# Layer 0's expert scatter in a two-layer transformer kernel: one fp32 product per token block, or two float32r products of a split row

## The chip, the cores and the metric

The kernel runs on one core of a Trainium2 chip, as one program and one launch. The metric is device microseconds of one execution. Engine names are those of the profile: PE is the matmul engine, PEld its weight loads, DVE the vector engine, ACT the scalar engine, POOL the GpSimd engine, SP the engine that issues most plain DMAs.

## What is computed

Two transformer layers over x of shape (8, 512, 128), with adaptive layer norms. Layer 0 is softmax attention and an expert layer in which each expert takes its own best tokens; layer 1 is linear attention and a top-2 expert layer. The change is in layer 0's expert layer:

```python
scores = jnp.einsum('ntd,ed->nte', x, gate_w)
probs = jax.nn.softmax(scores, axis=-1)
g, m = jax.lax.top_k(probs.transpose(0, 2, 1), k)      # 8 experts, k = 128 of 512 tokens
xin = x[batch_idx, m]
h = jnp.einsum('nekd,edf->nekf', xin, w1)
h = jax.nn.gelu(h, approximate=False)
h = jnp.einsum('nekf,efd->nekd', h, w2)
out_tok = g[..., None] * h
out = jnp.zeros((n, t, d), dtype=x.dtype).at[batch_idx, m].add(out_tok)
```

and x becomes x + gb * out, with gb a gate per batch and feature.

## The kernel before, in words

The program has three parts. `program_attention` does layer 0's attention for all 8 batches and the choice of each expert's tokens. `program_experts` begins with a pipeline of stages, one batch wide, in which three batches are in work at once: layer 0's experts of batch nn = b + 2, layer 1's attention of batch nxt = b + 1, and layer 1's routing of batch b. After it come 72 tiles of layer 1's experts and an output part. The change touches only the pipeline.

A stage is cut into Q = 32 slots, and the order is written by hand. On each engine a table `work[q]` lists functions by slot; slot after slot they are issued in the order in which they were appended, and the engine runs them in that order. Expert e of the stage occupies slots from 4e on:

- PE: `hidden0(e+1)` in slot 4e (4 products of 128x128x128, L1852), `output0(e)` in slot 4e+1 (4 products into bank `tb`, L1860), `scatter(e-1)` in slot 4e+2 (4 products, L1870). The last expert's `scatter(7)` runs in slot 2 of the next stage. An fp32 product stands in the trace as two weight loads and two matmuls, so 4 products are x8.
- ACT: `gelu0(e+1)` in slot 4e+1 (L1374).
- DVE: `spread_picks(e)` in slot 4e makes a 128x512 matrix of zeros and ones (L1549): which token each of the expert's 128 rows belongs to. `save_y0(e)` in slot 4e+2 reads `tb`, multiplies by the token weight and the gate and writes `y0[e % 2]` (L1558).

`scatter(e)` multiplies, for each of 4 token blocks, a 128x128 quarter of `spread` (as weights) by `y0` and accumulates over the 8 experts in bank `a2`. `start_b` (DVE, slot 3, L1523) adds that bank to x, and takes the statistics of layer 1's first norm (L1490, L1495).

Other work that the prediction speaks of, with its slots: on PE `norm2_T` in 5 (L1821), `logits` in 7 and `shared` in 8 (both L1826), `norm1_T` in 9 (L1821), `values` in 15 (L1826), `ranks` in 18 (L1971 to L1976, waits for `combT_ready`), `contexts` in 19 (L1914). On ACT `save_hTf` in 6 (L1413; `logits` waits for it), `shift_1` in 10 (L1380), `exp_router` in 11 (L1418), `q_positive` in 13 (L1392), `gelu_shared` in 15 (L1422), `exp_qk` and `save_v1` in 16 (L1396 to L1403), `save_combT` in 18 (L1427). ACT loads a table each time it goes from gelu to exp or back. On DVE `norm_f` in 31 (L1541), `q_negative` in 14 and `k_negative` in 15.

The stages differ in what runs beside the experts. The first has the experts alone, the second also layer 1's attention, and in both DVE does one round of `take_best` per expert (slot 4e+1: MAX8, FIND_INDEX8, MATCH_REPLACE8 over 512 columns) for the last two batches. Six more have experts, attention and routing; two after these have no layer 0 experts.

Of the kernel before, what the change touches and what calls it, by code (L numbers as in the profile page):

```python
# [14 lines left out]
F32 = mybir.dt.float32  # L15
BF16 = mybir.dt.bfloat16
F32R = mybir.dt.float32r
I32 = mybir.dt.int32
U32 = mybir.dt.uint32
ALU = mybir.AluOpType  # L20
# [3 lines left out]
P = 128  # L24
B, T, D = 8, 512, 128
# [4 lines left out]
E, F = 8, 512  # L30
# [934 lines left out]
def program_experts(nc, io, keep, scratch, held):  # L965
# [4 lines left out]
    with ctx:  # L970
        def sb(name, shape, dt=F32):
            return ctx.enter_context(nc.sbuf_tensor(name, shape, dt))
# [4 lines left out]
        def sem(name):  # L977
            held.append(nc.alloc_semaphore(name=name))
            return held[-1]
# [10 lines left out]
        def column(name, rows=P):  # L990
# [18 lines left out]
        xg = sb("xg", [P, E, D])  # L1009
        xin = sb("xin", [P, E, KSEL])  # L1010
        hid0 = [sb(f"hid0_{i}", [P, NF, KSEL]) for i in range(2)]
        spread = [sb(f"spread{i}", [P, T]) for i in range(2)]
        y0 = [sb(f"y0_{i}", [P, D]) for i in range(2)]

        st_b = sb("st_b", [P, NT, 6])
        mv_b = sb("mv_b", [P, NT, 2])
# [90 lines left out]
        a2 = pb("a2", [P, T])  # L1107
# [16 lines left out]
        g_filled, xin_ready, z0_filled, hid0_ready, spread_ready, y0_filled, y0_ready, sc_filled, x0_ready = (  # L1124
            sem(n) for n in "g_filled xin_ready z0_filled hid0_ready spread_ready y0_filled y0_ready sc_filled "
            "x0_ready".split())

        stb_done, mvb_done, rb_step, rsb_ready, xhb_ready, hT1_filled, hT1_ready = (
            sem(n) for n in "stb_done mvb_done rb_step rsb_ready xhb_ready hT1_filled hT1_ready".split())
# [55 lines left out]
        def quarter(t):  # L1185
            return slice(P * t, P * (t + 1))
# [170 lines left out]
        def _(act):  # L1357
            def iteration(it):
                b, nxt, nn = it.own, it.own + 1, it.own + 2
# [10 lines left out]
                def gelu0(m, e):  # L1370
                    act.wait_ge(z0_filled, E * m + e + 1)
                    if e >= 2 or not (isinstance(m, int) and m == 0):
                        act.wait_ge(y0_filled, E * m + e - 1)
                    nc.scalar.activation(hid0[e % 2][:].rearrange("p n k -> p (n k)"), ps_h[e % 2][:], ACT.Gelu  # L1374
                                         ).then_inc(hid0_ready, 1)

                def shift_1():
                    act.wait_ge(hT1_filled, nxt + 1)
                    act.wait_ge(q1_filled, nxt)
                    nc.scalar.activation(hT1[:], b0_[:], ACT.Identity, scale=scale1[:, 1, 0, bass.ds(nxt, 1)],  # L1380
                                         bias=mod[:, 1, SHIFT_A, bass.ds(nxt, 1)]).then_inc(hT1_ready, 1)
# [47 lines left out]
                work = {q: [] for q in range(Q)}  # L1429
                if it.ffn:  # L1430
                    if not it.attn:
                        work[0] += [lambda: gathered(0, 0), lambda: gathered(0, 1), lambda: gelu0(0, 0)]
                    for e in range(E - 1):
                        work[4 * e + 1].append(lambda e=e: gelu0(nn, e + 1))
                    if it.ffn_next:
                        work[24].append(lambda: gathered(nn + 1, 0))
                        work[29].append(lambda: gelu0(nn + 1, 0))
                        work[31].append(lambda: gathered(nn + 1, 1))
# [46 lines left out]
        def _(dve):  # L1485
# [32 lines left out]
            def iteration(it):  # L1518
                b, nxt, nn = it.own, it.own + 1, it.own + 2
# [32 lines left out]
                def save_y0(e):  # L1552
                    dve.wait_ge(y0_filled, E * nn + e + 1)
                    if e >= 2 or not (isinstance(nn, int) and nn == 0):
                        dve.wait_ge(sc_filled, E * nn + e - 1)
                    dve.wait_ge(gate0_in, 16)
                    settle(dve)
                    nc.vector.scalar_tensor_tensor(y0[e % 2][:], tb[:, 0:D], weight_of[:, nn, e:e + 1],  # L1558
                                                   gate0[:, nn, :], ALU.mult, ALU.mult).then_inc(y0_ready, 1)

                def take_last(n):
                    if n == 0:
# [166 lines left out]
                if it.ffn and not it.route:  # L1729

                    for n in range(ROUNDS // 2):
                        work[4 * n + 1].append(lambda n=n: take_last(ROUNDS // 2 * (b + 2) + n))
                    if it.attn:
                        work[29] += [place_last, save_earlier]
                        work[31].append(keep_last)
                for q in range(Q):
                    for f in work[q]:
                        f()
# [79 lines left out]
        def _(pe):  # L1818
# [10 lines left out]
            def iteration(it):  # L1829
# [32 lines left out]
                    last.then_inc(y0_filled, 1)  # L1862

                def scatter(m, e):
                    pe.wait_ge(y0_ready, E * m + e + 1)
                    pe.wait_ge(spread_ready, E * m + e + 1)
                    if e == 0:
                        pe.wait_ge(x0_ready, m)
                    for t in range(NT):
                        last = nc.tensor.matmul(a2[:, quarter(t)], spread[e % 2][:, quarter(t)], y0[e % 2][:],  # L1870
                                                start=(e == 0 and t == 0), stop=(e == E - 1), skip_group_check=True)
                    last.then_inc(sc_filled, 1)

                def picks_T(which, n):
# [298 lines left out]
```

## Time and profile before

| | |
|---|---|
| median of 3 runs | 1170.81 us (1170.74 to 1175.88) |
| the profiled execution, its own time | 1174.08 us |
| its span from first to last instruction | 1172.4 us |
| mean granted TensorE clock | 0.901 |
| PE / PEld / DVE / ACT / POOL busy | 84% / 53% / 65% / 49% / 38% |
| pipeline stages with layer 0 experts | about 588 to 888 us |

A row of the trace's timeline gives start, duration, engine, line, operation, output and inputs, and in brackets how long the engine had been idle and which instruction released it. Matmuls overlap: the mean duration of one (278 ns for L1870) is not its cost in a stream. The cost is the distance from the start of one group to the start of the next.

### The profile page before, as it was taken

The numbers are of one execution on the slowest core, as the hardware profiler recorded it, in microseconds if no ns is written. First come the engines' busy times: TensorE is split into PE (matmuls) and PEld (weight loads), VectorE is DVE, ScalarE is ACT, GpSimd is POOL, SyncE is SP. The second block draws the span as 40 slices with busy tenths as digits, with TensorE's granted clock in tenths as the row PEclk, the third lists the DMA queues.
The fourth block names the chain that finished last, engine by engine and source line by source line (L and its number), as shares of the span: only waits on it lengthen the run. The fifth ranks groups of instructions, "written<-read, shape, count | busy, mean of one in ns | idle before, by whom it ended". The sixth has DMA issues, their size and how long they took to land.

```text
span 1172.4 us, 21238 instructions
## 1 busy us (share of the span) xinstructions
PE 981.7 (84%) x6249; PEld 616.0 (53%) x6249; DVE 766.4 (65%) x1912; ACT 579.6 (49%) x1225; POOL 444.3 (38%) x625
## 2 busy tenths in 40 slices
PE   4699999999899999994198999999996539999764
PEld 3133333333233333332197888889885439999621
DVE  3668787878687878896188756665665336656333
ACT  1057676767576767771023533552453116666421
POOL 4030414131222222121324565665534336666532
PEclk9569999999899999996599999999998559999876
DMA  4432323232232324510600010100101012222232
GB/s 141 140 120 75 132 72 131 74 128 76 100 105 97 106 96 108 186 49 10 277 19 19 20 31 27 31 26 22 33 8 48 18 33 68 65 68 68 82 92 75
DMA packets 55645, 90.11 MB, mean 77 GB/s; under 512 B 9393, under 2 KB 40539, under 8 KB 54902
## 3 DMA queue, kind: packets, MB, share of 16 engines
q1 hardware_dynamic: 45942, 58.68, 17.5%
q0 software_dynamic: 9600, 30.24, 7.2%
q8 instruction: 42, 0.69, 0.3%
q14 instruction: 61, 0.50, 0.1%
HBM read 49.62 MB, written 39.30 MB: 76 GB/s over the span
## 4 chain that ended last, share of the span: by engine, by line
PE 34%; DVE 6%; DMA 3%; issue 3%; POOL 3%; ACT 3%; SPq 0%; DVEq 0%; ACTq 0%; POOLq 0%
PE a L2030 6%; PE tb L1860 5%; PE a L1852 4%; PE a L1870 4%; PE b_ L2039 3%; PE c L1826 2%; PE a L2039 2%; PE b_ L1826 2%; DMA weights<-back_dram 1%; DMA xg<-tokens_dram,row_of 1%; PE b_ L1922 1%; PE b_ L1821 1%; ACT L1418 1%; PE b_ L1914 1%; POOL rows_dram L1303 1%
## 5 line engine op out<-in xcount | busy, mean ns | idle before, releaser
L630 DVE TENSOR_REDUCE nmax<-ps_s 128x1 f32<-128x512 f32 x512 | 324.8, 683 | 87.7 <-PE ps_s L795 86.5
L524 ACT ACTIVATE p_ring<-ps_t 128x512 f32<-128x512 f32 x512 | 287.2, 597 | 141.6 <-PE ps_t L806 138.1
L817 PE MATMUL ps_av<-p_ring,v_ext 128*32 128x512 f32 x1024 | 138.8, 615 | 0.0
L795 PE MATMUL ps_s<-weights 72*128 72x512 bf16 x256 | 108.3, 427 | 19.5 <-DMA weights<-q_parts_dram 15.6
L1466 ACT ACTIVATE weights<-a,wtile 128x128 f32<-128x128 f32 x288 | 82.3, 368 | 49.5 <-PE a L2030 49.5
L1330 POOL DMA_INDIRECT back_dram<-weights,target x72 | 84.0, 1167 | 57.8 <-DVE weights L1783 51.9
L806 PE MATMUL ps_t<-weights 75*128 75x512 bf16 x256 | 102.0, 398 | 2.6 <-ACT p_ring L524 1.5
L806 PE MATMUL ps_t<-q_stack,k_stack 75*128 75x512 bf16 x256 | 96.7, 382 | 3.9 <-ACT p_ring L524 2.0
L795 PE MATMUL ps_s<-k_stack,q_stack 72*128 72x512 bf16 x256 | 98.1, 383 | 1.3 <-DVE nmax L630 1.3
L1374 ACT ACTIVATE hid<-a 128x512 f32<-128x512 f32 x64 | 38.2, 597 | 112.5 <-PE a L1852 112.3
L1303 POOL DMA_INDIRECT rows_dram<-hrow,slot x64 | 63.2, 988 | 64.5 <-DVE slot L1690 46.1
L1852 PE MATMUL a<-xin,weights 128*128 128x128 f32 x512 | 74.7, 292 | 7.8 <-ACT xin L1366 7.8
L2030 PE MATMUL a<-hTt,wtile 128*128 128x128 f32 x576 | 78.4, 280 | 3.1 <-ACT hTt L1457 3.1
L1261 POOL DMA_INDIRECT xg<-tokens_dram,row_of x64 | 63.4, 990 | 38.0 <-DVE row_of L1513 18.9
L795 PEld LDWEIGHTS ps_s<-weights 72*128 72x128 bf16 x256 | 26.0, 102 | 97.1 <-DVE nmax L630 55.3
L2030 PEld LDWEIGHTS a<-hTt,wtile 128*128 128x128 f32 x576 | 71.5, 195 | 5.6 <-ACT hTt L1457 4.8
L1769 DVE COPY wtile<-wall 128x1028 f32 x72 | 56.7, 787 | 27.1 <-issue 26.5
L1852 PEld LDWEIGHTS a<-xin,weights 128*128 128x128 f32 x512 | 65.4, 200 | 16.7 <-issue 8.6
L1860 PE MATMUL tb<-weights,hid 128*128 128x128 f32 x512 | 72.0, 286 | 2.5 <-DVE y L1558 1.8
L1860 PEld LDWEIGHTS tb<-weights,hid 128*128 128x128 f32 x512 | 66.6, 202 | 7.5 <-issue 4.7
L455 POOL CAST m_parts<-nmax 128x16 bf16<-128x16 f32 x32 | 6.3, 198 | 167.1 <-DVE nmax L630 167.1
L1870 PE MATMUL a<-y,spread 128*128 128x128 f32 x512 | 68.6, 278 | 0.7 <-DVE y L1558 0.7
(286 smaller groups left out, 1681.2 us busy)
## 6 DMA issues: line engine op xcount, KB each, us to landing
rows_dram<-wmod POOLq DMA_DIRECT2D x8, 2145.0 KB
q_parts_dram<-q_parts SPq DMA_DIRECT2D x40, 128.0 KB, 2.4
xt<-rows_dram SPq DMA_DIRECT2D x72, 65.0 KB, 1.8
weights<-k_parts_dram SPq DMA_DIRECT2D x16, 288.0 KB
weights<-q_parts_dram SPq DMA_DIRECT2D x16, 288.0 KB
k_stack<-k_parts_dram SPq DMA_DIRECT2D x16, 288.0 KB
q_stack<-q_parts_dram SPq DMA_DIRECT2D x16, 288.0 KB
wall<-in_wall SPq DMA_DIRECT2D x1, 4112.0 KB, 20.7
```

Of the source, the lines that this page charges most:

```text
L524: nc.scalar.activation(probs[:, u % RING, :], ps_t[u % TBANKS][:], ACT.Exp, scale=HD ** -0.5).then_inc(exp_done, 1)
L630: nc.vector.tensor_reduce(nmax[:, js, n:n + 1], ps_s[u % SBANKS][:], AX.X, ALU.max, negate=True).then_inc(max_done, 1)
L795: nc.tensor.matmul(ps_s[u % SBANKS][:], q_stack[par][0:STACK, h, quarter(t)], k_stack[par][0:STACK, h, :], start=True, stop=True).then_inc ...
L806: nc.tensor.matmul(ps_t[u % TBANKS][:], k_stack[par][0:STACK + PARTS, h, quarter(t)], q_stack[par][0:STACK + PARTS, h, :], start=True, sto ...
L817: last = nc.tensor.matmul(ps_av[32 * g:32 * (g + 1), :], v_ext[par][:, t, HG * j + g, :], probs[:, (HG * k + g) % RING, :], start=(t == 0) ...
L1303: nc.gpsimd.indirect_dma_start(out=scratch["rows"].ap(), out_offset=bass.IndirectOffsetOnAxis(ap=slot[:, k, t:t + 1], axis=0), in_=hrow[:, ...
L1330: nc.gpsimd.indirect_dma_start(out=scratch["back"].ap(), out_offset=bass.IndirectOffsetOnAxis(ap=target[j % YT][:, 0:1], axis=0), in_=yt[j ...
L1466: last = nc.scalar.activation(hid1[j % 2][:, n, :], ps_z[j % 2][:, quarter(n)], ACT.Gelu, bias=wtile[j % WT][:, 2 * F + n:2 * F + n + 1])
L1852: last = nc.tensor.matmul(ps_h[e % 2][:, quarter(f)], w1_0[:, e, quarter(f)], xin[:, e, :], start=True, stop=True)
L1860: last = nc.tensor.matmul(tb[:, 0:D], hid0[e % 2][:, f, :], w2_0[:, e, f, :], start=(f == 0), stop=(f == NF - 1))
L1870: last = nc.tensor.matmul(a2[:, quarter(t)], spread[e % 2][:, quarter(t)], y0[e % 2][:], start=(e == 0 and t == 0), stop=(e == E - 1), ski ...
L2030: last = nc.tensor.matmul(ps_z[j % 2][:, quarter(n)], wtile[j % WT][:, quarter(n)], hTt[j % 2][:], start=True, stop=True)
```

## The change

Each expert's 128x128 rows `y0` are split in two float32r tiles. ACT copies `y0` into the first (`high_y0`), which rounds it; DVE subtracts that from `y0` into the second (`low_y0`). `spread` becomes float32r too (zeros and ones). The scatter makes two float32r products per token block, high and low, into the same quarter of `a2`, and waits for the low part. In the compiled program a float32r product is one weight load and one matmul, and an fp32 product is two of each.

```diff
-        spread = [sb(f"spread{i}", [P, T]) for i in range(2)]
+        spread = [sb(f"spread{i}", [P, T], F32R) for i in range(2)]
         y0 = [sb(f"y0_{i}", [P, D]) for i in range(2)]
+        y0_parts = [sb(f"y0_parts{i}", [P, 2, D], F32R) for i in range(2)]
...
+                def high_y0(e):
+                    act.wait_ge(y0_ready, E * nn + e + 1)
+                    nc.scalar.copy(y0_parts[e % 2][:, 0, :], y0[e % 2][:]).then_inc(y0_high_ready, 1)
...
                         work[4 * e + 1].append(lambda e=e: gelu0(nn, e + 1))
+                    for e in range(E):
+                        work[4 * e + 2].append(lambda e=e: high_y0(e))
...
+                def low_y0(e):
+                    dve.wait_ge(y0_high_ready, E * nn + e + 1)
+                    nc.vector.tensor_tensor(y0_parts[e % 2][:, 1, :], y0[e % 2][:],
+                                            y0_parts[e % 2][:, 0, :].bitcast(F32), ALU.subtract
+                                            ).then_inc(y0_low_ready, 1)
...
+                if it.ffn:
+                    for e in range(E):
+                        work[4 * e + 3].append(lambda e=e: low_y0(e))
...
                 def scatter(m, e):
-                    pe.wait_ge(y0_ready, E * m + e + 1)
+                    pe.wait_ge(y0_low_ready, E * m + e + 1)
                     pe.wait_ge(spread_ready, E * m + e + 1)
...
                     for t in range(NT):
-                        last = nc.tensor.matmul(a2[:, quarter(t)], spread[e % 2][:, quarter(t)], y0[e % 2][:],
-                                                start=(e == 0 and t == 0), stop=(e == E - 1), skip_group_check=True)
+                        for c in range(2):
+                            last = nc.tensor.matmul(a2[:, quarter(t)], spread[e % 2][:, quarter(t)],
+                                                    y0_parts[e % 2][:, c, :], start=(e == 0 and t == 0 and c == 0),
+                                                    stop=(e == E - 1 and c == 1), skip_group_check=True)
```

The instructions of PE keep their order. On ACT and DVE the two new ones stand at hand-written places. In the changed kernel's rows line numbers are higher: by 2 to 6 on ACT, by 8 to 14 on DVE.

ACT, first routed stage, slots 1 to 10, before (`hid` is `gelu0`, `hT_f` is `save_hTf`, `hT` is `shift_1`):

```order
L1374 ACTIVATE hid_1<-a 128x512
L1374 ACTIVATE hid_0<-a 128x512
L1413 COPY hT_f<-c 128x512
L1374 ACTIVATE hid_1<-a 128x512
L1380 ACTIVATE hT<-b_,mod,scale 128x512
```

and now (`y_parts` is `high_y0`):

```order
L1376 ACTIVATE hid_1<-a 128x512
L1381 CAST y_parts<-y_0 128x128
L1376 ACTIVATE hid_0<-a 128x512
L1381 CAST y_parts<-y_1 128x128
L1419 COPY hT_f<-c 128x512
L1376 ACTIVATE hid_1<-a 128x512
L1381 CAST y_parts<-y_0 128x128
L1386 ACTIVATE hT<-b_,mod,scale 128x512
```

The casts of expert 1 and expert 2, which wait for DVE, now stand directly ahead of `hT_f` and `hT`.

ACT, the same stage, slots 13 to 18, before (`q_pos` is `q_positive`, `sh` is `gelu_shared`, `combT` is `save_combT`):

```order
L1392 ACTIVATE q_pos<-b_,small 128x512
L1422 ACTIVATE sh<-sh 128x512
L1396 ACT_TABLE_LOAD
L1396 ACTIVATE q_exp<-q_exp 128x512
L1398 ACTIVATE k_exp<-k_exp 128x512
L1403 COPY v<-b_ 128x4x128
L1374 ACT_TABLE_LOAD
L1374 ACTIVATE hid_1<-a 128x512
L1427 COPY combT<-c 8x512
```

and now:

```order
L1398 ACTIVATE q_pos<-b_,small 128x512
L1381 CAST y_parts<-y_1 128x128
L1428 ACTIVATE sh<-sh 128x512
L1402 ACT_TABLE_LOAD
L1402 ACTIVATE q_exp<-q_exp 128x512
L1404 ACTIVATE k_exp<-k_exp 128x512
L1409 COPY v<-b_ 128x4x128
L1376 ACT_TABLE_LOAD
L1376 ACTIVATE hid_1<-a 128x512
L1381 CAST y_parts<-y_0 128x128
L1433 COPY combT<-c 8x512
```

Expert 3's cast stands ahead of `sh` and the table load, and expert 4's ahead of `combT`.

DVE, the first routed stage, slots 2 to 8, now (`y_0` and `y_1` are `save_y0`, `y_parts` is `low_y0`, `x` with `st_b` and `mv_b` is `start_b`); before, the order is the same without the two `y_parts` rows:

```order
L1566 SCALAR_TENSOR_TENSOR y_0<-tb,weight_of,gate 128x128
L1521 TENSOR_TENSOR row_of<-token_of,tokens 128x8
L1531 TENSOR_TENSOR x<-a,x 128x512
L1498 BN_STATS st_b<-x 128x6 x4
L1503 BN_AGGR mv_b<-st_b 128x2 x4
L1571 TENSOR_TENSOR y_parts<-y_0,y_parts 128x128
L1557 TENSOR_SCALAR spread<-tokens,token_of 128x512
L1566 SCALAR_TENSOR_TENSOR y_1<-tb,weight_of,gate 128x128
L1571 TENSOR_TENSOR y_parts<-y_1,y_parts 128x128
L1557 TENSOR_SCALAR spread<-tokens,token_of 128x512
```

Expert 0's subtraction comes only after the whole of `start_b`.

## Rows read from the trace of the kernel before

**Rows 1.** The page: busy time, granted clock in 40 slices, the chain by line.

```profile
PE 981.7 (84%) x6249; PEld 616.0 (53%) x6249; DVE 766.4 (65%) x1912; ACT 579.6 (49%) x1225; POOL 444.3 (38%) x625
...
PEclk9569999999899999996599999999998559999876
...
PE a L2030 6%; PE tb L1860 5%; PE a L1852 4%; PE a L1870 4%; PE b_ L2039 3%; PE c L1826 2%; PE a L2039 2%; PE b_ L1826 2%; DMA weights<-back_dram 1%; DMA xg<-tokens_dram,row_of 1%; PE b_ L1922 1%; PE b_ L1821 1%; ACT L1418 1%; PE b_ L1914 1%; POOL rows_dram L1303 1%
```

**Rows 2.** Three stretches: start, end, length; PE, PEld, DVE, ACT, POOL busy; clock.

```profile
589.20:612.40 23.20, 21.30 (x188) 20.82 (x187) 21.55 (x57) 6.03 (x10) 8.37 (x8) 1.00 0.09 24
612.40:653.20 40.80, 35.95 (x295) 33.10 (x294) 35.16 (x94) 14.27 (x21) 16.45 (x20) 1.00 0.05 14
653.20:855.60 202.40, 188.28 (x1488) 173.47 (x1487) 127.61 (x404) 88.21 (x125) 121.36 (x140) 0.96 0.09 27
```

**Rows 3.** Timeline of PE, a routed stage, slots 6 to 8.

```profile
775.06 1.06 PE L1870 MATMUL a<-y,spread 128*128 128x128 f32 x8
775.97 1.06 PE L1826 MATMUL c<-small,hT_f 128*128 128x8 f32 x8
776.89 1.14 PE L1852 MATMUL a<-xin,weights 128*128 128x128 f32 x8
```

**Rows 4.** Timeline of PE, the same stage, slots 18 and 19.

```profile
793.10 1.05 PE L1870 MATMUL a<-y,spread 128*128 128x128 f32 x8
793.99 0.18 PE L1971 MATMUL c<-picked_b,earlier_b 128*128 128x32 bf16 x1
794.01 0.22 PE L1974 MATMUL c<-picked_b,ones_b 128*128 128x24 bf16 x3
794.12 1.14 PE L1914 MATMUL b_<-v,k_phi 128*128 128x129 f32 x8
```

**Rows 5.** Groups of instructions by line, as on the page.

```profile
L1457 ACT COPY hTt<-tb 128x128 f32<-128x128 f32 x36 | 10.2, 282 | 17.1 <-PE tb L2022 17.1
L1594 DVE TENSOR_TENSOR context<-b_,small 128x128 f32<-128x128 f32 x8 | 2.3, 285 | 0.7 <-PE b_ L1914 0.7
```

**Rows 6.** Timeline of DVE, the first stage, one expert.

```profile
594.63 0.33 DVE L1558 SCALAR_TENSOR_TENSOR y<-tb,weight_of,gate 128x128 f32<-128x128 f32 x1
594.89 0.47 DVE L1549 TENSOR_SCALAR spread<-tokens,token_of 128x512 f32<-128x512 f32 x1
...
597.32 0.33 DVE L1558 SCALAR_TENSOR_TENSOR y<-tb,weight_of,gate 128x128 f32<-128x128 f32 x1
```

**Rows 7.** Timeline, a routed stage, slots 3 to 6.

```profile
775.29 0.38 DVE L1495 BATCH_NORM_AGGREGATE mv_b<-st_b 128x2 f32<-128x6 f32 x4
775.33 0.59 ACT L1413 COPY hT_f<-c 128x512 f32<-128x512 f32 x1 [1.69 <-PE c L1821]
775.59 0.47 DVE L1549 TENSOR_SCALAR spread<-tokens,token_of 128x512 f32<-128x512 f32 x1
775.98 0.34 DVE L1558 SCALAR_TENSOR_TENSOR y<-tb,weight_of,gate 128x128 f32<-128x128 f32 x1
```

**Rows 8.** Timeline, a later routed stage, the same slots.

```profile
856.20 0.34 DVE L1558 SCALAR_TENSOR_TENSOR y<-tb,weight_of,gate 128x128 f32<-128x128 f32 x1
856.64 1.00 PE L1826 MATMUL c<-small,hT_f 128*128 128x8 f32 x8
```

**Rows 9.** Timeline, slots 10 and 11 of the stage of rows 7.

```profile
780.02 0.35 DVE L1558 SCALAR_TENSOR_TENSOR y<-tb,weight_of,gate 128x128 f32<-128x128 f32 x1 [1.08 <-PE tb L1860]
780.44 0.78 ACT L1380 ACTIVATE hT<-b_,mod,scale 128x512 f32<-128x512 f32 x1 [1.78 <-PE b_ L1821]
```

**Rows 10.** Timeline, slots 14 to 18 of the same stage.

```profile
786.92 0.35 DVE L1558 SCALAR_TENSOR_TENSOR y<-tb,weight_of,gate 128x128 f32<-128x128 f32 x1
787.97 0.63 ACT L1396 ACTIVATE q_exp<-q_exp 128x512 f32<-128x512 f32 x1 [0.33 <-DVE q_exp L1578]
791.67 0.57 ACT L1427 COPY combT<-c 8x512 f32<-8x512 f32 x1
793.48 0.35 DVE L1558 SCALAR_TENSOR_TENSOR y<-tb,weight_of,gate 128x128 f32<-128x128 f32 x1 [0.96 <-PE tb L1860]
```

More of the change, by code:

```diff
@@ L1126, in program_experts @@
             "x0_ready".split())
+        y0_high_ready, y0_low_ready = sem("y0_high_ready"), sem("y0_low_ready")
         stb_done, mvb_done, rb_step, rsb_ready, xhb_ready, hT1_filled, hT1_ready = (
```

## The prediction, as it was put on record

> **What bounds the kernel now.** I read the page first [rows 1]: PE is busy 84% of the span, and no other engine comes near. The change lies in the 300 us from 588 to 888. The table of stretches [rows 2] says what rules there. In the six routed stages (653 to 856 and on to 888) PE is busy 188.3 of 202.4 us and DVE 127.6: PE rules, and any wait put into its queue costs its own length. In the first stage PE has 21.3 of 23.2 us and DVE 21.55, in the second 35.95 and 35.16 of 40.8: two engines are level. The timeline shows what that means in the first stage [rows 6]: DVE has no idle time between the products of an expert, and its period, 597.32 - 594.63 = 2.69 us, is the same as PE's three groups of 0.89. There DVE work is path, too.
>
> **The matmuls: cost 0.** A scatter takes 775.97 - 775.06 = 0.91 us for 8 pairs of weight load and matmul [rows 3], 0.89 to 0.91 elsewhere (794.0 - 793.10) [rows 4]: 112 ns a pair. The group behind it, also 8 pairs with 128-column fp32 weights, moves only 8 columns instead of 128, and takes 776.89 - 775.97 = 0.92 us. So 112 to 115 ns is what a 128-column fp32 weight load costs in the stream, however little the matmul does. [...] I take 112 ns a pair: nothing won, nothing lost. The lower bound is the bf16 row [rows 4]: 5 pairs (L1971, three of L1974, one of L1976) between 793.99 and 794.12, 26 ns each; 8 x 26 = 0.21 us a scatter, 0.68 less, and 64 x 0.68 = 44 us. The upper bound: the pair costs twice as much, 0.89 us more for each scatter, 57 us. The nearest row is the 8-column one, hence 0.
>
> [...]
>
> **The two new instructions.** A 128x128 copy on ACT takes 0.28 us, and so does a two-operand 128x128 operation on DVE, whose successor can start some 0.2 us after it, both read at other places [rows 5]. 64 of each are 18 us on either engine. Over most of ACT's time that is idle time. The cost is in the places where the new waits stand, because ACT and DVE run strictly in the order written.
>
> *First stage, DVE is path.* `low_y0(e)` follows `save_y0(e)` directly, but needs ACT's copy. From the start of `save_y0`: 0.35 to its end, 0.04 to ACT, 0.28 copy, 0.04 back, then some 0.25 for the subtraction: the next instruction starts 1.0 us after it, where it now starts after 0.26 [rows 6]. That is 0.75 us more for each expert and 6.0 for eight. DVE has 23.2 - 21.55 = 1.65 us of idle time to give, so about +4.
>
> *Second stage.* The same 6.0 us, against 40.8 - 35.16 = 5.6 us of idle time, of which only part lies where it can be used (DVE waits there for results of the attention too). About +4.
>
> *Routed stages, slots 3 to 7.* Expert 0's subtraction stands behind `start_b`, whose last row begins at 775.29 and lets `spread` start at 775.59 [rows 7]. The subtraction takes that place and ends near 775.87, but `scatter(0)` started at 775.0 [rows 3]. Then `spread` and `save_y0(1)` follow 0.2 us later than now (775.98), to 776.55; ACT's copy of expert 1 runs to 776.88, and only behind it comes `hT_f`, which ran at 775.33 and is now 776.92 to 777.50. `logits` starts at 777.55 in place of 775.97: +1.6 us of idle PE. In another stage [rows 8] the same reckoning starts from `save_y0` at 856.20 + 0.2 and puts `logits` at 857.75 in place of 856.64: +1.1. I count four stages like that and two like rows 7: 4 x 1.1 + 2 x 1.6 = 7.6 us.
>
> *Slot 10.* ACT's copy of expert 2 can start at 780.41, when `save_y0` ends, and `hT` stood at 780.44 [rows 9]. PE waits behind a chain from `hT` through a table load and DVE. +0.28 us, six times, and once in the second stage: 2.
>
> *Slots 14 to 18.* The copy of expert 3 waits for `save_y0` at 786.92 + 0.35; behind it are now `sh` (0.63) and the exp table load (1.28), which before ran during that wait. So `q_exp` starts at 789.5 and not at 787.97 [rows 10]. PE does not need those exponentials until `contexts` at 794.12 [rows 4], so I cost this at nothing; if that cover were gone it would be 1.5 us a stage. But `combT` comes behind the copy of expert 4, which waits for `save_y0` until 793.83: 794.15, and `combT` ends at 794.75 where it ended at 792.24. `ranks` stood at 793.99 and waits for it: +0.8 us. In the last of these stages, where ACT is then the later one, 1.6. Together 5 x 0.8 + 1.6 = 5.6.
>
> *Slot 31.* `low_y0(7)` comes after `norm_f`; its reader is in slot 2 of the next stage and stands later than that. Small shifts, 0.1 us a stage: 0.6.
>
> Sum: 0 + 4 + 4 + 7.6 + 2 + 5.6 + 0.6 = 23.8, **+24 us**. The profiled execution took 1174.1 us and would take 1198; it is 0.3% above the median of the three runs, and I put the sum on the median: 1170.8 + 24 = **1195 us**. A measurement of this kernel tells 0.5%, 6 us, from no change.
>
> Not in the sum is the clock. [...] A group of 8 pairs at half the clock takes up to 0.9 us more, and one or two more such groups in each of six stages would be 5 to 11 us.
>
> **The rivals.**
>
> *B, the weight load is not the limit of a float32r pair, and the kernel gets faster.* [...] As a mechanism of this kernel: the scatter's stretch shrinks towards the bf16 rows. The chain holds L1870 with 4% of the span [rows 1], 47 us, at 0.91 some 52 of the 64 scatters. At 56 ns a pair (half of 112) it is 52 x 0.45 = 23 us back, and 1172 results. At the bound of 26 ns it is 52 x 0.68 = 35 us, and 1170.8 + 24 - 35 = 1160: faster than before. It turns at 112 - 24,000 / (52 x 8) = 54 ns a pair. For it: bf16 weights do load fast here [rows 4]. Against it: float32r weights are four bytes wide, like those of the 8-column row.
>
> *C, a float32r pair costs more than an fp32 pair at 128 columns.* At twice the price, 52 x 0.89 = 46 us more: 1241. No row shows a float32r product, so nothing excludes it.
>
> *D, the waits are absorbed.* The routed stages have 14 us of PE idle time in five stages [rows 2]; if the new waits fall into it instead of adding to it, only the DVE-bound stages pay, and it is 1175 to 1180.
>
> *E, the same sum with the clock added*, and the exponentials' cover gone (6 x 1.5): 1195 + 11 + 9 = 1215, rounded up to 1216.
>
> **How the numbers follow.** The forecast, with its terms off by a third either way, 1187 to 1204: 0.55. E, up to 1216: 0.15. D: 0.13. B: 0.10, of which half ends within 0.5% of before, 0.03 below and 0.02 above. C: 0.07. Faster by over 0.5% needs B at its far end: 0.03. Within 0.5%: half of B, and a little of D: 0.07. Slower: 0.90. The range leaves out C and B, and takes in D and E: 1175 to 1216.
>
> **What would show it.** Right: L1888 with 512 matmuls and groups of 8 still 0.89 us apart; in the first stage a DVE period near 3.4 us; in a routed stage PE idle ahead of `scatter(0)` and `logits`, released by `y_parts` and `hT_f`, 1 to 2 us together, and ahead of `ranks`, released by `combT`; `hT_f` directly behind a cast. Wrong: groups of L1888 at 0.45 us (B) or 1.8 (C); a routed stage that is still 40.4 us long (D).

## The result: slower by 4%, twice the forecast

| | before | changed |
|---|---|---|
| median of 4 runs each | 1173.35 us (1170.74 to 1176.06) | 1219.26 us (1212.09 to 1223.39) |
| ratio, 95% interval | | 1.0385 (1.0326 to 1.0443) |
| the profiled execution, its own time / span | 1174.08 / 1172.4 us | 1219.26 / 1217.6 us |
| mean granted clock | 0.901 | 0.886 |

The sign was right; the time lies 24 us above the forecast of 1195 and just outside the range, which ended at 1216. Of these 24 us, 22 are the change itself, +46 where +24 was forecast; the rest is the base, 1170.8 us in the forecast and 1173.35 in this comparison. The changed kernel was measured a second time, beside some of the experiments below:

> The changed kernel once more, unaltered, to stand beside these on the same chip: 1212 to 1224 us.

It gave 1220.11 us, ratio 1.0405 (1.0367 to 1.0443).

The page of the changed kernel, against [rows 1]:

```profile
PE 1007.2 (83%) x6249; PEld 637.1 (52%) x6249; DVE 773.4 (64%) x1976; ACT 595.2 (49%) x1289; POOL 447.5 (37%) x625
...
PEclk9579999999999999985898889889898559999976
...
L1888 PE MATMUL a<-y_parts,spread 128*128 128x128 f32 x512 | 72.8, 287 | 7.8 <-DVE y_parts L1571 7.7
...
L1381 ACT CAST y_parts<-y 128x128 fp32r<-128x128 f32 x64 | 19.1, 298 | 118.1 <-DVE y L1566 118.1
```

PE has the same 6249 matmuls and 25.5 us more busy time; ACT and DVE have the 64 new instructions each. In the clock's row the nines of the routed stages have become eights and nines. Both of the mistakes of the forecast show in the next view.

**By stage.** Each stage is measured from one start of `start_b` to the next. The rows give start, end and length, then busy time of PE, PEld, DVE, ACT and POOL, the granted clock, and the DMA's share and rate. First the second stage and the six routed ones of the changed kernel:

```profile
618.02:661.83 43.81, 36.28 (x263) 32.77 (x263) 32.76 (x99) 15.28 (x27) 16.89 (x20) 0.89 0.05 13
661.83:708.11 46.28, 40.83 (x309) 37.43 (x309) 27.51 (x89) 19.76 (x34) 24.64 (x28) 0.92 0.08 24
708.11:754.07 45.96, 40.23 (x291) 36.83 (x290) 25.74 (x89) 19.47 (x33) 23.93 (x29) 0.89 0.08 24
754.07:801.44 47.37, 41.00 (x311) 37.44 (x310) 27.32 (x89) 20.11 (x34) 25.91 (x29) 0.93 0.08 24
801.44:848.23 46.79, 39.99 (x288) 36.58 (x288) 26.35 (x90) 19.04 (x32) 23.43 (x28) 0.89 0.08 23
848.23:894.50 46.27, 41.09 (x298) 37.69 (x298) 25.93 (x87) 19.61 (x33) 24.96 (x29) 0.89 0.08 23
894.50:935.31 40.81, 34.36 (x265) 31.01 (x264) 23.77 (x85) 16.67 (x28) 16.90 (x20) 0.96 0.05 15
```

The same cut of the kernel before, first, middle and last of its seven:

```profile
613.90:652.37 38.47, 33.62 (x273) 30.77 (x272) 34.03 (x90) 13.46 (x20) 16.39 (x20) 1.00 0.06 15
...
773.51:813.50 39.99, 37.16 (x292) 34.22 (x293) 25.55 (x81) 17.17 (x25) 23.32 (x28) 0.96 0.09 27
...
853.73:889.36 35.63, 32.33 (x265) 29.54 (x263) 23.09 (x78) 14.83 (x21) 14.88 (x19) 1.00 0.05 17
```

Summed over the six routed stages, before had 237.0 us with PE busy 219.6 and idle 17.4. The changed kernel has 273.5 with PE busy 237.5 and idle 36.0. So of 36.5 us, 18.6 are new idle time and 17.9 are the same matmuls taking longer, at clocks of 0.89 to 0.96 where they had 0.96 to 1.00. The second stage gave 5.3 more (2.7 idle, 2.6 busy), and the first ended 4.1 later. That is 45.9. Behind the last `start_b` the two kernels take 283.0 and 282.3 us.

The profile of the second measurement has 276.3 us in the six stages, PE busy 237.5 and idle 38.8: from one execution to another these sums move by some 3 us.

**What PE waited for** in the six routed stages of the changed kernel: us in total, times, longest.

```profile
PE b_ L1843 <- DVE q_exp L1592: 11.8, 6, 2.5
PE a L1888 <- DVE y_parts L1571: 7.1, 6, 3.5
PE a L1869 <- ACT xin L1368: 5.0, 5, 1.1
PE b_ L1838 <- DVE att L1620: 4.2, 6, 0.8
PE c L1990 <- issue: 2.7, 5, 0.6
PE c L1843 <- ACT hT_f L1419: 2.2, 6, 0.4
PE b_ L1915 <- ACT hT L1386: 1.9, 6, 0.4
```

and before, all that it shows above 1 us:

```profile
PE b_ L1826 <- DVE q_exp L1578: 5.4, 6, 1.0
PE a L1852 <- ACT xin L1366: 5.0, 5, 1.1
PE b_ L1821 <- DVE att L1606: 3.9, 6, 0.6
```

The waits for `y_parts`, `hT_f`, `hT` and in front of `ranks` (L1990) are the new ones that the prediction named. The largest growth, 6.4 us, is that for `q_exp`, which it did not have. One more row of this kernel and one of before show what a pause is followed by. PE, slots 4 to 10 of a routed stage; compare [rows 3], where the same three groups are 0.91 and 0.92 us apart:

```profile
801.72 0.60 PE L1838 MATMUL c<-ident,hrow 128*128 128x128 f32 x4
803.85 1.11 PE L1888 MATMUL a<-y_parts,spread 128*128 128x128 f32 x8 [1.53 <-DVE y_parts L1571]
805.32 1.59 PE L1843 MATMUL c<-small,hT_f 128*128 128x8 f32 x8 [0.36 <-ACT hT_f L1419]
806.76 2.05 PE L1869 MATMUL a<-xin,weights 128*128 128x128 f32 x8
808.61 1.91 PE L1843 MATMUL c<-small,hT_f 128*128 128x128 f32 x8
810.32 1.92 PE L1877 MATMUL tb<-weights,hid 128*128 128x128 f32 x8
812.02 0.83 PE L1838 MATMUL b_<-ident,xh_b 128*128 128x128 f32 x4
```

After 1.53 + 0.36 us of waiting, three groups of eight pairs start 1.85, 1.71 and 1.70 us apart, where 0.92 is usual. The granted clock of that stretch, and of the one after the wait for `q_exp` at 821.98:

```profile
802.00:806.00 4.00, 2.11 (x16) 1.73 (x14) 3.17 (x15) 0.78 (x2) 2.06 (x3) 0.96 0.00 0
806.00:810.00 4.00, 4.00 (x20) 4.00 (x20) 1.33 (x6) 0.60 (x1) 3.09 (x4) 0.50 0.15 42
810.00:814.00 4.00, 3.82 (x24) 3.68 (x24) 1.25 (x4) 1.16 (x3) 3.08 (x4) 0.69 0.21 55
...
818.00:822.00 4.00, 1.71 (x15) 1.47 (x14) 3.59 (x14) 1.21 (x3) 0.00 (x0) 1.00 0.00 0
822.00:826.00 4.00, 4.00 (x21) 3.45 (x21) 2.49 (x8) 3.95 (x6) 1.27 (x1) 0.59 0.00 0
```

0.50 is half of the full clock, for the whole stretch. It comes behind the stretch in which PE waited, not in it, and PE is then fully busy at half speed. The kernel before had one such place in its stage, behind `q_exp`, with 0.70 from 788 to 792.

### The profile page after: what moved, and what is told of

It is laid out like the page before. It is cut to its first block, busy times and chain, and to the rows that moved or that the text cites. A ratio compares the mean times of both kernels' runs of the same rounds, so it can differ in the third digit from the quotient of the medians.

```text
span 1217.6 us, 21369 instructions
## 1 busy us (share of the span) xinstructions
PE 1007.2 (83%) x6249; PEld 637.1 (52%) x6249; DVE 773.4 (64%) x1976; ACT 595.2 (49%) x1289; POOL 447.5 (37%) x625
## 4 chain that ended last, share of the span: by engine, by line
PE 32%; DVE 9%; issue 4%; ACT 3%; DMA 3%; POOL 2%; DVEq 0%; SPq 0%; ACTq 0%; POOLq 0%
PE a L2049 6%; PE a L1869 4%; PE tb L1877 4%; PE b_ L2058 3%; PE a L1888 3%; PE c L1843 3%; PE a L2058 2%; PE b_ L1843 2%; DMA weights<-back_dram 1%; DMA xg<-tokens_dram,row_of 1%; PE b_ L1941 1%; PE b_ L1933 1%; ACT L1424 1%; DVE y L1566 1%; POOL rows_dram L1305 1%
## 5 line engine op out<-in xcount | busy, mean ns | idle before, releaser
L1869 PE MATMUL a<-xin,weights 128*128 128x128 f32 x512 | 82.6, 312 | 9.8 <-ACT xin L1368 9.8
L1869 PEld LDWEIGHTS a<-xin,weights 128*128 128x128 f32 x512 | 72.2, 218 | 20.0 <-issue 10.4
L1888 PE MATMUL a<-y_parts,spread 128*128 128x128 f32 x512 | 72.8, 287 | 7.8 <-DVE y_parts L1571 7.7
L1877 PE MATMUL tb<-weights,hid 128*128 128x128 f32 x512 | 75.9, 296 | 3.4 <-DVE y L1566 3.4
L1381 ACT CAST y_parts<-y 128x128 fp32r<-128x128 f32 x64 | 19.1, 298 | 118.1 <-DVE y L1566 118.1
L1877 PEld LDWEIGHTS tb<-weights,hid 128*128 128x128 f32 x512 | 70.4, 211 | 8.9 <-issue 7.7
L1566 DVE SCALAR_TENSOR_TENSOR y<-tb,weight_of,gate 128x128 f32<-128x128 f32 x64 | 22.1, 345 | 83.1 <-PE tb L1877 82.4
```

What stands on the lines that cost most here:

```text
L1869: last = nc.tensor.matmul(ps_h[e % 2][:, quarter(f)], w1_0[:, e, quarter(f)], xin[:, e, :], start=True, stop=True)
L1877: last = nc.tensor.matmul(tb[:, 0:D], hid0[e % 2][:, f, :], w2_0[:, e, f, :], start=(f == 0), stop=(f == NF - 1))
```

## The experiments

Twelve kernels ran, the changed one again among them. The diffs are against the changed kernel unless a line says otherwise. The kernel before measured 1172.3 to 1172.5 us beside each set.

**The products alone.** `y0` is made float32r, the copy and the subtraction are gone, and both products of a block take `y0`: the rows are added twice, rounded.

```diff
-        y0 = [sb(f"y0_{i}", [P, D]) for i in range(2)]
+        y0 = [sb(f"y0_{i}", [P, D], F32R) for i in range(2)]
...
-                    for e in range(E):
-                        work[4 * e + 2].append(lambda e=e: high_y0(e))
...
-                    pe.wait_ge(y0_low_ready, E * m + e + 1)
+                    pe.wait_ge(y0_ready, E * m + e + 1)
...
-                                                    y0_parts[e % 2][:, c, :], start=(e == 0 and t == 0 and c == 0),
+                                                    y0[e % 2][:], start=(e == 0 and t == 0 and c == 0),
```

> The changed scatter without its split: save_y0 writes y0 as float32r, and the scatter makes both float32r products with it, so that no copy, no subtraction and no new wait is left (each expert's rows, rounded, are added twice; the output is not the reference's). Theory W (the waits, with the clock drops that follow them, are the whole loss; a float32r pair costs what an fp32 pair costs): 1167 to 1177 us, groups of 8 pairs 0.89 us apart, one low-clock stretch in a routed stage as before. Theory L (the lighter matmuls keep the granted clock down, or cost more in the stream): 1185 to 1200 us, with low-clock stretches in a routed stage though nothing new is waited for.

Measured: 1172.82 us, ratio 1.0001 (0.9983 to 1.0018). PE's timeline:

```profile
769.09 1.09 PE L1883 MATMUL a<-y,spread 128*128 128x128 f32 x8
770.08 1.06 PE L1838 MATMUL c<-small,hT_f 128*128 128x8 f32 x8
```

These two groups are 0.99 us apart; in four of the six routed stages the same two are 0.92 or 0.93, and so are most distances behind a group of L1883. Behind one of L1870 before, most are 0.89 or 0.90: 115 to 116 ns for a float32r pair against 111 to 112 for half of an fp32 product. Over 64 scatters that makes 2 us, which is as much as the interval of this ratio leaves open. The rest of the 46 us comes from the split.

**The waits alone.** Split and waits as in the change, but `spread` and the parts are fp32 and the scatter is one fp32 product of the first part (the second is computed and not used).

```diff
-                        for c in range(2):
-                            last = nc.tensor.matmul(a2[:, quarter(t)], spread[e % 2][:, quarter(t)],
-                                                    y0_parts[e % 2][:, c, :], start=(e == 0 and t == 0 and c == 0),
-                                                    stop=(e == E - 1 and c == 1), skip_group_check=True)
+                        last = nc.tensor.matmul(a2[:, quarter(t)], spread[e % 2][:, quarter(t)],
+                                                y0_parts[e % 2][:, 0, :], start=(e == 0 and t == 0),
+                                                stop=(e == E - 1), skip_group_check=True)
```

> The split with its copy, subtraction and waits, all in fp32, and the scatter with one fp32 product of the copied rows as before (the copy is exact, the subtraction gives zeros and is not used). Theory W: 1212 to 1224 us, as slow as the changed kernel, with the second low-clock stretch behind scatter(0) in the routed stages. Theory L: 1190 to 1205 us, without that stretch.

Measured: 1211.61 us, ratio 1.0321 (1.0282 to 1.0361), 0.4 us below the range of theory W. Its routed stages take 270.2 us, PE busy 230.8 and idle 39.4. So the waits by themselves, with the products of before, make some 39 of the 46 us. Of the other 7, the float32r pairs account for 2 as above; the rest is not explained. In the profiles, whose executions took 1216.37 and 1219.26 us, this kernel has 3.4 us more idle and 6.7 less busy time in the routed stages than the changed one.

**The split on DVE alone.** The rounding copy moves from ACT to DVE, directly behind `save_y0`, followed by the subtraction.

```diff
+                def split_y0(e):
+                    dve.wait_ge(y0_ready, E * nn + e + 1)
+                    nc.vector.tensor_copy(y0_parts[e % 2][:, 0, :], y0[e % 2][:]).then_inc(y0_high_ready, 1)
...
+                        work[4 * e + 2] += [lambda e=e: save_y0(e), lambda e=e: split_y0(e)]
```

> The changed kernel with both parts made by DVE directly behind save_y0: ACT gets no new instruction, and start_b comes after the split. Theory W: the waits of hT_f, combT and scatter(0) are gone; left are some 0.5 us of DVE work for each expert, of which the first two stages pay 3 us each and the six routed ones 0.5 to 1.2 each: 1178 to 1190 us. Theory L: 1200 us or more, since the products are the same as in the changed kernel.

Measured: 1190.86 us, ratio 1.0153 (1.0114 to 1.0191), just above what was expected. DVE does 64 operations more, and the kernel is 29 us faster than the changed one, so the work itself is not what costs. Two things changed at once, though: the split no longer passes through ACT's queue, and expert 0's part now stands ahead of `start_b`. The routed stages take 251.9 us, no less than the 252.9 of the next kernel, which keeps ACT and only moves two functions. What the passage through ACT costs by itself is therefore not shown; the places in the order are what costs in the routed stages.

**Slots 3 to 7 mended.** `low_y0(0)` goes ahead of `start_b`, and `high_y0(1)` behind `save_hTf`.

```diff
-                        work[4 * e + 2].append(lambda e=e: high_y0(e))
+                        work[4 * e + 2 + (e == 1)].append(lambda e=e: high_y0(e))
...
+                        if e == 0:
+                            work[3].insert(0, lambda: low_y0(0))
```

> The changed kernel with two functions moved: expert 0's subtraction ahead of start_b, and expert 1's copy behind save_hTf (slot 7). Theory W: in each routed stage the 1.1 to 1.6 us of waiting goes and, with it, the low-clock stretch behind it (some 3 us): 1188 to 1200 us. If that clock drop has another cause than this wait (theory L), only the wait goes: 1208 to 1214 us.

Measured: 1195.01 us, ratio 1.0165 (1.0108 to 1.0222), 24.5 us below the changed kernel. The routed stages fell from 273.5 to 252.9 us, 9.3 of it idle time and 11.3 busy time. The waits for `y_parts` and `hT_f` that went make 5.8 us, where 7.6 was predicted, and the wait for `q_exp` fell by 4.0; with them went about their own length in low-clock stretches.

**Slots 14 to 18 mended too.** `high_y0(3)` and `high_y0(4)` go behind `save_v1` and `save_combT`, `low_y0(3)` two slots later. This diff is against the kernel just above.

```diff
-                        work[4 * e + 2 + (e == 1)].append(lambda e=e: high_y0(e))
+                        if e not in (3, 4):
+                            work[4 * e + 2 + (e == 1)].append(lambda e=e: high_y0(e))
...
+                if it.ffn:
+                    work[16].append(lambda: high_y0(3))
+                    work[18].append(lambda: high_y0(4))
...
-                            work[4 * e + 3].append(lambda e=e: low_y0(e))
+                            work[4 * e + 3 + 2 * (e == 3)].append(lambda e=e: low_y0(e))
```

> As the kernel with slots 3 to 7 mended (1195 us), and in addition expert 3's copy goes behind save_v1 (slot 16, its subtraction to slot 17), and expert 4's behind save_combT. Theory W: combT no longer waits for save_y0(4), which gives back 0.8 us of PE's waiting before ranks in five stages and 1.6 in one, 5.6 us, and perhaps a part of the clock that is lost there: 1184 to 1190 us. If the waits of slots 14 to 18 were hidden, 1192 to 1198.

Measured: 1195.16 us (1190.71 to 1199.5), ratio 1.0208 (1.017 to 1.0245). In the profiled execution, the fastest of the four, the wait in front of `ranks` is gone and the routed stages take 244.0 us; in the median there is no gain over the kernel just above, and the time is that of the second expectation, in which these waits were hidden. Whether they cost anything stays open.

**A pause alone.** The kernel before, with one more wait in front of `logits`, for POOL's `rs_b`, in the six routed stages (this diff is against the kernel before); nothing is added on ACT or DVE.

```diff
                     pe.wait_ge(hTf_ready, b + 1)
+                    if it.ffn:
+                        pe.wait_ge(rsb_ready, nxt + 1)
                     pe.wait_ge(slot_ready, b)
```

> The kernel before with nothing but a pause on PE: in the six routed stages logits also waits for POOL's rs_b, which comes 0.9 to 1.4 us after the time at which logits now starts. No float32r, no new instruction on ACT or DVE. If only the pause counts: 6 x 1.1 = 6.6 us, 1177 to 1181 us. If a pause of that length at that place also costs a low-clock stretch (theory W with the clock): some 3 us more a stage, 1190 to 1200 us, and a granted clock of 0.5 in the 4 us behind it.

Measured: 1198.29 us, ratio 1.0227 (1.0198 to 1.0257). PE's waits, then a timeline behind one of the pauses:

```profile
PE b_ L1826 <- DVE q_exp L1578: 11.9, 6, 2.8
PE c L1826 <- issue: 7.5, 6, 2.1
```

```profile
788.97 1.03 PE L1826 MATMUL c<-small,hT_f 128*128 128x8 f32 x8 [1.25 <-issue]
789.85 1.74 PE L1852 MATMUL a<-xin,weights 128*128 128x128 f32 x8
791.38 1.91 PE L1826 MATMUL c<-small,hT_f 128*128 128x128 f32 x8
```

Six pauses, 7.5 us together, made the routed stages 27.3 us longer: idle time grew by 14.0 (the 7.5, and 6.5 more for `q_exp`, 5.4 before), busy time by 13.3. From 790 to 794, behind the pause of 1.25 us in these rows, the granted clock is 0.57. This is the pattern of the change without the change.

**One product.** `y0` float32r, one float32r product a block: the low part is left out, so the rows are rounded. As with the products alone, the copy, the subtraction and the new wait are gone; the diff shows only the product.

```diff
-                        for c in range(2):
-                            last = nc.tensor.matmul(a2[:, quarter(t)], spread[e % 2][:, quarter(t)],
-                                                    y0_parts[e % 2][:, c, :], start=(e == 0 and t == 0 and c == 0),
-                                                    stop=(e == E - 1 and c == 1), skip_group_check=True)
+                        last = nc.tensor.matmul(a2[:, quarter(t)], spread[e % 2][:, quarter(t)], y0[e % 2][:],
+                                                start=(e == 0 and t == 0), stop=(e == E - 1), skip_group_check=True)
```

> One float32r product per token block with y0 written as float32r by save_y0 (no low part, no copy, no new wait; the rows are rounded). It halves the pairs of a scatter and so prices the pair. If a pair costs 112 ns in the stream (weight load), a scatter takes 0.45 us and some 52 of 64 lie on the path: 1172 - 23 = 1149 us, 1145 to 1158. [...] If the time freed on PE is given back to the clock gate as pauses, 1160 to 1170.

Measured: 1171.66 us, ratio 0.9992 (0.9975 to 1.0009). PE's timeline, with a wait, and later the group of four pairs:

```profile
744.69 2.04 PE L1838 MATMUL b_<-small,latent 33*128 33x128 f32 x8 [3.02 <-DVE q_exp L1590]
...
760.98 0.64 PE L1882 MATMUL a<-y,spread 128*128 128x128 f32 x4
761.45 1.11 PE L1838 MATMUL b_<-wo_gated,attT 128*128 128x128 f32 x8
```

The group takes 0.47 us (761.45 - 760.98) instead of 0.91: 117 ns a pair, with half the pairs. Over 64 scatters that is 28 us of PE's work, and none of it is gained. In the routed stages PE is busy 14.6 us less and idle 15.2 more; the wait for `q_exp` rose from 5.4 to 13.2 us, and waits for `hT` (3.4) and `hT_f` (1.8) are new. My expectation took the scatters' share of the chain as what a shorter scatter gives. It does not: PE arrives earlier at a result of DVE that comes no earlier. DVE and POOL beside that wait show why it comes even later:

```profile
741.70 1.93 DVE L1675 SCALAR_TENSOR_TENSOR picked<-ahead,picked 128x32 f32<-128x32 f32 x1
741.88 1.68 POOL L1289 TENSOR_TENSOR x<-x,gate_att  x4
```

This 128x32 operation takes 0.18 to 0.53 us in five of its eight stages, and 1.90 to 1.93 in three, each time beside POOL's four additions.

**POOL's additions later, in four kernels.** The four additions of `gate_att` to x move behind POOL's addition into `q_exp`, the same edit in each:

```diff
-                    for t in range(NT):
-                        last = nc.gpsimd.tensor_tensor(x_all[:, nxt, t, :], x_all[:, nxt, t, :],
-                                                       gate_att1[:, 1, nxt, :], ALU.add)
-                    last.then_inc(xb1_ready, 1)
...
                     nc.gpsimd.tensor_tensor(q_exp[:], q_exp[:], q_pos[:], ALU.add).then_inc(qphi_ready, 1)
+                    for t in range(NT):
+                        last = nc.gpsimd.tensor_tensor(x_all[:, nxt, t, :], x_all[:, nxt, t, :],
+                                                       gate_att1[:, 1, nxt, :], ALU.add)
+                    last.then_inc(xb1_ready, 1)
```

In the kernel with one product:

> The kernel with one float32r product per block (1172 us), with POOL's four additions to x (x<-x,gate_att) moved behind its addition to q_exp. In the routed stages of one_product PE saved 0.45 us a scatter, yet waited 3.0 us (before: 1.05) for q_exp, because a DVE operation of the routing chain was stretched from 0.2 to 1.9 us beside these POOL additions, and a low-clock stretch followed. Theory P (the collision with POOL gave the gain back): 1150 to 1160 us. If the gain is lost elsewhere (the chain from hT to q_exp is the bound whatever PE does): 1168 to 1174.

Measured: 1167.61 us, ratio 0.9951 (0.9929 to 0.9973). That lies between the two expectations, close to the one without a gain. The wait for `q_exp` fell from 13.2 to 8.7 us, but the one for `hT` stayed at 3.4, and in the routed stages PE is still idle for 27.9 us, 17.4 before. So the collision ate a part of the gain, and for the rest PE comes earlier to results that come no earlier. In the kernel before:

> The kernel before with the same move of POOL's additions alone, as the control: it has the collision outside its path in most stages (spread and hrow are stretched), so theory P expects little, 1166 to 1174 us.

Measured: 1171.73 us, ratio 1.0004 (0.9985 to 1.0022). In the kernel with both waits mended:

> The two-product kernel with slots 3 to 7 and 14 to 18 mended (1195 us), with the same move of POOL's additions. If its routed stages, still some 1.2 us longer each than before, are held by that collision: 1183 to 1190 us. If the rest of its loss sits in the first two stages (DVE-bound, some +10 us) and in the copy ahead of hT: 1192 to 1198.

Measured: 1191.46 us, ratio 1.0154 (1.0127 to 1.018), between the two expectations and not told apart from 1195.16 by these intervals; its routed stages take 244.9 us, 244.0 without the move. And in the changed kernel itself, where the wait for `q_exp` was to be explained:

> The changed kernel with POOL's four additions to x moved behind its addition into q_exp. In the changed kernel PE waits 11.8 us for q_exp in the six routed stages (5.4 before the change), from the start of hT to the start of q_exp pass 7.6 to 8.3 us (6.5 to 6.9 before), and one DVE operation on picks or probabilities lasts 1.3 to 2.1 us beside these additions. Theory P (the pause made early in the stage lets POOL's additions fall ahead of q_exp, where they stretch DVE's chain): hT to q_exp is back at 6.5 to 6.9 us, the wait for q_exp falls by some 6 us to 5 to 6, and with it goes the low-clock stretch behind it, which costs 0.5 to 1 us of PE busy a stage, so 1219.5 - 6.4 - (3 to 6) = 1207 to 1210. Theory N (the wait for q_exp has grown for another reason, such as ACT's later table loads or the low clock itself): the additions only move, the wait stays near 11.8 us, and the time is 1216 to 1223. The waits for y_parts, hT_f and ranks stay in both.

Measured: 1209.71 us (1207.64 to 1213.55), ratio 1.0333 (1.0293 to 1.0373): within theory P's range, some 10 us below the two medians of the changed kernel (1219.26 and 1220.11); by the ratios, 1.0385 and 1.0405, it is 6 to 8 us, and the intervals touch. PE's waits in its routed stages, the two largest:

```profile
PE a L1888 <- DVE y_parts L1571: 7.5, 6, 3.5
PE b_ L1843 <- DVE q_exp L1592: 7.1, 6, 1.6
```

The wait for `q_exp` went from 11.8 to 7.1 us, and the others stayed within 0.4. The rows of the changed kernel that it undid, DVE and POOL:

```profile
815.44 1.69 POOL L1289 TENSOR_TENSOR x<-x,gate_att  x4
815.83 1.36 DVE L1654 TENSOR_TENSOR prob<-lexp,linv 128x32 f32<-128x32 f32 x1
...
821.10 0.74 DVE L1592 TENSOR_SCALAR q_exp<-b_,small 128x512 f32<-128x512 f32 x1
```

and of the kernel before:

```profile
787.19 0.74 DVE L1578 TENSOR_SCALAR q_exp<-b_,small 128x512 f32<-128x512 f32 x1
787.55 1.69 POOL L1287 TENSOR_TENSOR x<-x,gate_att  x4
```

POOL's queue runs at its own pace from the head of the stage, eight gathers and then these additions, and PE's pauses do not hold it up: the additions in these two fences begin 14.0 us after the `start_b` of their stage (801.44 and 773.51), with the change and without. In the five stages that have these gathers the additions began, before the change, between 0.1 us ahead of the start of `q_exp` and 1.5 behind it, when the chain towards it was over. Now that chain is later by the pause and by the low clock, the additions fall 2.3 to 5.7 us ahead of `q_exp`, and from `hT` to `q_exp` pass 7.6 to 8.3 us instead of 6.5 to 6.9; in three of the five stages one operation of the chain stands at 1.3 to 2.1 us in the trace. With the additions moved it is 6.5 to 7.3 us. The kernel with pauses alone shows the same: there the additions begin 3.0 to 5.4 us ahead of `q_exp`, and the wait for it is 11.9 us. It is not the only road to that wait. With the split on DVE, where four of the six stages have the additions 0.1 us behind the start of `q_exp`, from `hT` to `q_exp` pass 7.6 us in these four, and PE waits 12.1 us for it in all six. That this comes from the operations added on DVE is argued, not tested.

## Why the prediction was right in its waits, and wrong in its time

- *The matmuls, cost 0*: right within 2 us. 1.0001 with the products alone, 115 to 116 ns a pair where 112 was taken, and 117 where half of them are left out. Rivals B and C are excluded. The weight loads of float32r (L1888) have a median of 192 ns, like those of fp32 before (L1870), where the bf16 ones of `ranks` (L1971 to L1976) have 96 to 100. No run shows how much work a float32r matmul does beside one of the two of an fp32 product; what the runs show is the pair in the stream, and it costs no less.
- *First stage, +4*: right. The scatters stand 3.34 to 3.56 us apart (596.42 - 592.86, 603.10 - 599.76), forecast 3.4, and the stage ended 4.1 us later. PE there, with the 0.93 us of a float32r scatter:

```profile
596.42 1.09 PE L1888 MATMUL a<-y_parts,spread 128*128 128x128 f32 x8
597.35 1.10 PE L1869 MATMUL a<-xin,weights 128*128 128x128 f32 x8
...
599.76 1.09 PE L1888 MATMUL a<-y_parts,spread 128*128 128x128 f32 x8
```

- *Second stage, +4*: 5.3 us. The idle part was 2.7; 2.6 came from a clock of 0.89 where it had been 1.00.
- *Slots 3 to 7, 7.6*: the mechanism was right, `hT_f` stands directly behind the cast, and `scatter(0)` and `logits` wait. By the waits it is 3.6 for `y_parts` (7.1 without the one of 3.5, below) and 2.2 for `hT_f`, 5.8 together; the kernel with these slots mended has 9.3 us less idle time, since the wait for `q_exp` shrinks too (7.8).
- *Slot 10, 2*: right for `hT` itself, 1.9.
- *Slots 14 to 18, 5.6*: mis-sized. The wait in front of `ranks` is 2.7 us, 0.64 at most a stage: `combT` came later as described, but PE came later too. The delay of the exponentials, costed at nothing, shows no wait of its own.
- *Slot 31, 0.6*: mis-sized. Behind the last of these stages nothing stands between, and `scatter(7)` waited 3.53 us for `low_y0(7)`, which stands behind `norm_f` and its wait of 1.43 us for POOL; before it waited 0.74 for `y`. That is 2.8.

```profile
934.17 1.11 PE L1888 MATMUL a<-y_parts,spread 128*128 128x128 f32 x8 [3.53 <-DVE y_parts L1571]
```

- *The wait for `q_exp`, not in the sum*: +6.4. The last experiment took away 4.7 of it with the collision on DVE; the other 1.7 is not explained. That is the one wait that the prediction did not see: it looked at what stands behind the new instructions in their queues, and not at what of POOL's would now fall on DVE's chain.

The waits of the routed stages come to 5.8 + 1.9 + 2.7 + 2.8 + 6.4 = 19.6 us by their rows, 18.6 by the stages, and 15.8 in the sum. So **the step that failed is the sentence that left the clock out of the sum**. It was estimated at 5 to 11 us, from one or two slow groups a stage, with no row that shows what a pause does to the clock; measured are 17.9 us in the routed stages and 2.6 in the second, about three slow groups behind the first wait of a stage and more behind that for `q_exp`. Of the 22 us by which the change was mis-sized, these 20.5 are the clock, 2.8 are the routed waits (18.6 against 15.8), and the waits of the first two stages came out 1.2 smaller (6.8 against 8). Rival E had the right mechanism, and added 9 us for exponentials that cost nothing in place of a clock twice as dear. The kernel with pauses alone has 13.3 us of slow matmuls for 14.0 us of new idle time, and the changed kernel 17.9 for 18.6, about one for one. That rate is no constant: it is 17.9 for 21.4 in the second profile of the changed kernel, 11.2 for 22.0 with the waits alone, 6.6 for 9.3 with slots 3 to 7 mended and 2.2 for 4.8 with both places mended, each figure good to some 3 us. With a rate of a half to one, the sum would have been 8 + 1.5 x 15.8 = 32 to 8 + 2 x 15.8 = 40, against 46. The prediction also reads 188.3 of 202.4 us as six stages; [rows 2] has five there, which changes none of its terms.

What stays open: 5 of the 7 us between the waits alone and the changed kernel; what sets how much slow work follows a pause; why the second mended kernel's shorter stages don't show in its median; and how much of the lost gain with one product is DVE's stretched chain and how much the clock.

## What to carry to other kernels

Cost a new wait on a full matmul engine at more than its length, here at some one and a half times to twice: where the trace shows a low granted clock after a pause, take the slow groups behind it into the sum, not beside it. A term for the new order must also look at the engines that do not wait, because their work now falls on other work than before. And the share of a line in the chain of waits is no measure of what shortening it gives; look at what the engine would wait for next.

## What the runs showed of the hardware

- Pauses of PE of 1.2 to 2.3 us were followed by stretches with a granted clock of 0.50 to 0.59 (changed kernel: 1.53 + 0.36 us, then 0.50, and 2.29 us, then 0.59; pauses alone: 1.25 us, then 0.57), and in sum the slow products behind them cost about half to all of the idle time again (11.2 for 22.0 us, 13.3 for 14.0, 17.9 for 18.6). In the changed kernel, behind pauses in the middle of the program, the routed stages lost 17.9 us beyond what they had lost before, 1.5% of the kernel.
- A float32r product with 128x128 weights is one weight load and one matmul, in the stream 115 to 116 ns in groups of eight (0.92 or 0.93 us) and 117 to 120 in groups of four (0.47 or 0.48), where half of an fp32 product takes 111 to 112 (0.89 or 0.90 for eight). So two of them cost what one fp32 product does to within 4%, and one costs about half.
- In the changed kernel four small DVE operations (L1654, L1663, L1665, L1674) lasted 1.26 to 2.07 us beside POOL's additions, with medians of 0.17 to 0.19 over their eight stages; moving the additions took away 4.7 us of PE's waits, and 6 to 10 us of time.
